# Moving the first tile's second mask ahead of the head means, and its product ahead of the head-mean product, in a macaron block on one core

## The reference

```python
x = x + 0.5 * ffn(layernorm(x))          # 8 experts, top 2 by softmax, capacity per expert
x = x + attn(layernorm(x))
x = x + 0.5 * ffn(layernorm(x))

# attn: 16 heads of 16 channels
q, k, v = split(x @ w_qkv.T)             # q and k are rotated and scaled by position
scores = (q @ k.T) * D ** -0.5 * decay_mask          # causal, gamma ** distance
y = scores @ v
mean, var = y.mean, y.var                # for each batch and head, over its 16 channels and all 1024 tokens
yn = (y - mean) / sqrt(var + eps) * gn_weight + gn_bias
out = (silu(x @ w_gated.T) * yn) @ w_proj.T
```

## Time and profile before

| | |
|---|---|
| median of 3 runs | 2312.23 us (2309.82 to 2313.85) |
| profiled execution | 2312.59 us, of which the span from first to last instruction is 2310.8 us |
| PE busy | 2170.1 us, 94% of the span |
| DVE busy | 1358.5 us, 59% |
| ACT busy | 1003.8 us, 43% |
| POOL busy | 1171.7 us, 51% |
| mean granted TensorE clock | 0.977 of full speed |

### The profile page before, as it was taken

How to read it: one execution, slowest core, us unless ns; L and a number is a source line. 1 busy time by engine, 2 the same in 40 slices (tenths; PEclk the granted TensorE clock), 3 DMA queues, 4 the chain that set the end, 5 groups by cost and what they waited for, 6 DMA issues and landing times.

```text
span 2310.8 us, 57931 instructions
## 1 busy us (share of the span) xinstructions
PE 2170.1 (94%) x22549; PEld 1907.2 (83%) x22549; DVE 1358.5 (59%) x3312; ACT 1003.8 (43%) x2149; POOL 1171.7 (51%) x911
## 2 busy tenths in 40 slices
PE   7869999999999997999999999849999999999998
PEld 6759999999999987777777777638999999999997
DVE  7755555555555552578778877645555555555553
ACT  4434434343434342446555555434344444444442
POOL 5755777735354533223344453454777654444443
PEclk9999999999999998999999999869999999999999
DMA  9523444434343424102211121123444443434432
GB/s 365 211 81 68 101 93 99 99 87 98 82 104 81 105 55 119 39 21 76 76 40 59 59 77 75 60 81 94 100 92 102 90 101 86 100 87 99 89 80 32
DMA packets 138440, 211.52 MB, mean 92 GB/s; under 512 B 34092, under 2 KB 114544, under 8 KB 132080
## 3 DMA queue, kind: packets, MB, share of 16 engines
q0 software_dynamic: 57344, 69.21, 17.9%
q1 hardware_dynamic: 80912, 139.72, 17.5%
HBM read 138.13 MB, written 72.88 MB: 91 GB/s over the span
## 4 chain that ended last, share of the span: by engine, by line
PE 52%; DVE 4%; issue 2%; ACT 1%; another core or an unknown queue 0%; POOL 0%; DMA 0%; POOLq 0%; DVEq 0%; ACTq 0%
PE bank L675 16%; PE bank L657 15%; PE bank L768 10%; PE bank L856 3%; PE bank L889 1%; PE bank L824 1%; PE bank L644 1%; PE bank L839 1%; PE bank L874 1%; PE bank L928 1%; PE bank L786 1%; DVE aw L1829 0%; DVE rt L1817 0%; DVE xnl L1803 0%
## 5 line engine op out<-in xcount | busy, mean ns | idle before, releaser
L1167 ACT ACTIVATE h<-bank 128x512 f32<-128x512 f32 x512 | 306.1, 598 | 850.9 <-PE bank L657 740.0
L1738 DVE CAST hh<-h 128x512 fp32r<-128x512 f32 x512 | 241.2, 471 | 692.6 <-ACT h L1167 578.8
L675 PE MATMUL bank<-w2h,hh 128*128 128x256 f32 x2048 | 579.1, 283 | 3.1 <-ACT yb L1185 3.1
L675 PE MATMUL bank<-w2h,hl 128*128 128x256 f32 x2048 | 573.7, 280 | 0.0
L675 PE MATMUL bank<-w2l,hh 128*128 128x256 f32 x2048 | 573.7, 280 | 0.0
L675 PEld LDWEIGHTS bank<-w2h,hh 128*128 128x128 f32 x2048 | 385.1, 188 | 45.4 <-ACT yb L1185 3.6
L675 PEld LDWEIGHTS bank<-w2h,hl 128*128 128x128 f32 x2048 | 384.8, 188 | 41.5
L675 PEld LDWEIGHTS bank<-w2l,hh 128*128 128x128 f32 x2048 | 385.2, 188 | 39.4
L657 PE MATMUL bank<-xh,w1h 128*128 128x512 f32 x1024 | 405.1, 396 | 2.0 <-issue 1.7
L657 PE MATMUL bank<-xh,w1l 128*128 128x512 f32 x1024 | 404.3, 395 | 0.0
L657 PE MATMUL bank<-xl,w1h 128*128 128x512 f32 x1024 | 404.1, 395 | 0.0
(11 more groups left out here) (215 smaller groups left out, 3305.0 us busy)
## 6 DMA issues: line engine op xcount, KB each, us to landing
stg<-in_L_ffn_w SPq DMA_DIRECT2D x64, 1024.0 KB
xb<-acc SPq DMA_DIRECT2D x9, 1024.0 KB
xa<-in_L_attn_x SPq DMA_DIRECT2D x8, 1024.0 KB, 14.4
xn_rows<-xa SPq DMA_DIRECT2D x8, 1024.0 KB
xn_rows<-xn_r SPq DMA_DIRECT2D x8, 1024.0 KB
xr<-acc SPq DMA_DIRECT2D x7, 1024.0 KB
out_rows<-xr SPq DMA_DIRECT2D x7, 1024.0 KB
slot_table<-pay,idx POOLq DMA_INDIRECT x256
```

The source lines that it names most:

```text
L675: product = pe.matmul(tile_sum(j, t, end), a[:, fj, t * P:(t + 1) * P], c[:, fj, :], start=(fj == 0 and i == 0 and (end or t % 2 == 0)), s ...
L1167: act.activation(h32[fj % 2][:], bank[fj % 2][:], ACT.Gelu_apprx_tanh).then_inc(f.gelu, 1)
L1738: dve.tensor_copy(hh[:, fj, :], h32[fj % 2][:]).then_inc(f.hh, 1)
```

## The change

Two calls change places, one on each of two engines. On PE `attend(n)` now stands ahead of `head_means(b - 1)`. On DVE `mask(n, 1)` now stands ahead of `channels(b - 1)`.

```diff
@@ def sequence(b), in the program of TensorE @@
                 turn(n + 1)
                 memory(n)
                 new_state(n + 1, 0)
+                attend(n)
                 head_means(b - 1)
-                attend(n)
                 residual_pair(b - 2, 2)
                 scores(n + 1, 0)
                 new_state(n + 1, 1)
@@ def sequence(b), in the program of VectorE @@
                 mask(n, 0)
                 channel_stats(n - 1)
                 front_stats(b + 1, 0)
+                mask(n, 1)
                 channels(b - 1)
-                mask(n, 1)
                 rotate(n + 2)
                 carry(n + 1, 0)
                 about_head(b - 1)
```

## The result

The changed kernel took 2324.44 us (median of 6 runs, 2319.77 to 2326.66), the kernel before 2310.61 us beside it (6 runs). The ratio is 1.0052, with a 95% interval of 1.0039 to 1.0065, so 9 to 15 us slower. The forecast was 2320.8 us, in a range of 2313.5 to 2327.

The account below looks back on a forecast made before the run. PE was taken to bound the kernel, other engines counting only where PE waits for them. Waits of 5.45 us at L907 plus 3.1 us of clock falls, 8.55 us, gave 2320.8 us, range 2313.5 to 2327.

Parts of the forecast that it names:

- The mask gains nothing: On DVE at batch start: the mask still starts 0.73 us after its scores (L856), gain 0, with DVE idle ahead.
- Channels in the open, 1.25 us: On DVE: channels now runs after the mask, where nothing hides it, and delays what is queued behind by 1.25 us.
- TensorE's half, 0: On PE: `attend(n)` 0.31 us earlier, head means some 0.8 us later, together taking what they took: 0.
- L1885 is held by L504: DVE's L1885 lasts until POOL's L504 ends, about 1.14 us instead of 0.16 us, before and after the change.
- the rule that was weighed: SBUF port rule: two-input Vector instructions block while GpSimd reads SBUF; without it, near 1 us of waits instead of 5.45.
- The waits, 5.45 us: PE's added waits for DVE at L907 in batches 1 to 7, each 1.25 us less the slack: 5.45 us.
- The slack: Time between L1888 and L907 above 0.22 us: 1.07, 0.80 and 1.35 us in batches 3, 5 and 6.
- The clock, two new falls behind L907, 3.1 us: PE's clock falls to half level after L907 in two more of five batches, 1.55 us each: 3.1 us.
- The rate taken: How often PE's clock falls after a wait or gap near L907: two in four, used to take two falls.
- The sum, 8.55 us: Whole kernel: waits of 5.45 us at L907 plus clock falls of 3.1 us, 8.55 us slower.
- Rival C: Waits at L907 swallowed by PE's larger slack or issue gaps: 2315 us if half goes, 2312 if all; chance 0.18.
- Rival B: Waits at L907 alone, the clock falling no more often: 2317.7 us, slower by 0.24%; chance 0.19.

Follow-up runs that it names:

- e1: DVE's half of the change alone (mask ahead of channels, TensorE's order as before) against the kernel before: 2324.27 us, ratio 1.0035.
- e2: TensorE's half of the change alone (`attend(n)` ahead of the head means, DVE as before) against the kernel before: 2318.57 us, ratio 1.0008.
- e4: The change, with POOL also waiting for L1888 before it starts `rotated(n + 2)` (L504), against the kernel before: 2321.97 us, ratio 1.0021.
- e8: The kernel before with only POOL made to wait for L1888 before `rotated(n + 2)`, against the kernel before: ratio 0.9994.
- e11: The same kernel as e4, timed again in another group against the kernel before: ratio 1.0019.
- e12: The same kernel as e8, timed again in another group against the kernel before: ratio 0.9998.
- e9: The kernel before, unaltered, timed against itself and profiled a second time: ratio 0.9997.
- e5: The change itself again on another chip (second comparison and second profile), against the kernel before: 2322.51 us, ratio 1.0035.
- e6: The change, with TensorE filling its wait at L907 with 8 unread transposes in seven batches, against the kernel before: 2322.29 us, ratio 1.0034.
- e3: The change, with `head_variances(b - 1)` moved behind `residual_pair(b - 2, 3)` and `project(n + 3)` on TensorE, against the kernel before: ratio 1.0062.

## Why the prediction was right, and where it was off

The direction was right, and so was the path by which TensorE comes to wait at L907. That the sum came close is in part luck, as the last points show.

- **The mask gains nothing.** Right: 0.74 us behind its scores, with 1.17 us of idle time of DVE ahead of it.
- **Channels in the open, 1.25 us.** Right, 1.21 measured. By e1 and e2 the loss is in this half, as far as the times can tell.
- **TensorE's half, 0.** Right in time (e2). That the two calls "take what they took" was off by 0.2 us a batch in favour of the new order, by e1's waits against those of the change. It only made the wait longer.
- **L1885 is held by L504.** Shown by e4, e8, e11 and e12 (0.16 us in every case) and by e2. For the size of the loss the rule that was weighed mattered as said: with the block gone the stretch from L856 to L907 went from 39.98 back to 34.67 us, and an undisturbed batch lost 0.19 us (4.75 for 4.56) where the rule's absence was priced at 0.2. The time of the kernel didn't follow as far: the prediction had near 1 us for that case, and e4 and e11 show 4 to 5.
- **The waits, 5.45 us.** Measured as the growth of that stretch: 5.07. The bare idle time grew by 7.3 us (7.8 less 0.5), more than forecast. The issue gaps of 0.7 to 1.0 us that stood ahead of L907 in the batches 3, 5 and 6 lie within the new waits or beside them now. The slack that I had taken from them came out as expected all the same: 5.71 against 5.57, 5.30 and 5.85 are 0.14, 0.41 and -0.13 us, where I had 0.18, 0.45 and 0.
- **The clock, two new falls behind L907, 3.1 us.** Two in the first profile (batches 5 and 7), three in the second (2, 4, 5), one in e1 (5). The estimate was good for this place. But the lost clock of the whole stretch from batch 1 grew by 6.9, 3.4 and 8.6 us in these three. Falls came at other places too, some of double length (the one of batch 1 among them), and this I had put at nothing. The rate taken, two in four, would also have given 2.5 of five and not two.
- **The sum, 8.55 us.** From batch 1 on the profile shows 8.0, but not as 5.45 and 3.1: the lost clock grew by 6.9, and the issue gaps shrank. The two misses went opposite ways. The median shows 13.8 in the first comparison and 9.2 in the second; the intervals reach from 4.9 to 15.0. The term missed is batch 0, 3.7 us in the first profile. It is a longer gap in TensorE's issue and a fall of the clock behind it, in instructions that didn't change. Since e4 and e11, one kernel, show it at 3.0 and at 1.3 us, the program's order doesn't fix it. Whether the order makes the long gap likelier stays open.

Rival C had something for it. The issue gaps of TensorE from batch 1 to the end of the stage went from 9.3 to 6.8 us, and those that stood between L856 and L907 were passed during the new waits. But the kernel before itself shows only 5.9 us in e9, so the sum alone proves nothing, and it came nowhere near to paying for the waits. Rival B, the waits alone, would have been 2317.7 us, below every execution of the first comparison. The interval of e5, 5 to 11 us, still contains its 5.45. Against it stands the clock of the executions, 0.9743 for 0.9762; but since e6 has that clock nearly back at the same time, the part of the falls in the loss isn't shown.

Two things stay open: the 4 to 5 us that e4 and e11 keep although their stretch to L907 is as before, and how much of the median is due to the falls, which e6 should have shown and didn't. No version clearly beats the kernel before.

## What to carry to other kernels

Before an instruction is moved up on its engine, look at what ends the wait of the one that moves: if its start stands at a fixed distance behind its releaser in every batch (here 0.73 us), the work ahead of it is free filling, and moving up only turns that work into delay for everything behind. A chain that crosses engines is priced where the bounding engine meets it (here 4.56 us from L856 to L907 became 5.71), not by the length of the moved work. And a product moved out of the way of a wait (e3) takes its bank along: see who claims that bank next.

## What the hardware showed that I had not expected

- A DVE instruction on 2 numbers per partition took 1.13 us beside a POOL instruction that reads SBUF, and 0.16 us without it. It only mattered once something waited for it.
- TensorE stood for 1.3 to 4.2 us in its own issue at one and the same instruction (L839, batch 0), on the same program with 1.3 in one profile and 3.0 in another. The traces show what ended these gaps. Beside the data they list packets of 16 KB, one at a time, on a queue of the kind "instruction". Of the changed kernel, from 975 to 990 us:

```profile
q1 hardware_dynamic: 1184, 2.10, 40.0%
q8 instruction: 2, 0.03, 1.0%
```

The first of the two ran from 982.58 to 983.53, and TensorE went on at 985.02. In the kernel before it ran from 980.14 to 981.08, and TensorE went on at 982.54. The 14 profiles have 66 issue gaps of TensorE over 0.6 us between 930 and 1500 us, and every one ended 1.25 to 1.59 us after such a packet had landed. So these gaps are, by all that the traces show, waits for TensorE's own program. Just ahead of the gap in batch 0 two loads of 1 MB start to move. In the nine profiles with a gap of 1.3 to 1.6 us the packet started 1.3 to 1.7 us after the first data of these loads, in the five with 3.0 to 4.2 us it started 3.2 to 4.3 us after it. Whether the loads hold the packet back, or it was asked for later, isn't shown.
- The clock's answer to the same stretch with the same wait differs from batch to batch: behind a wait of 1.3 us it fell in 3 of 6 batches in the first profile (one further fall, in batch 6, had no wait ahead of L907) and in 4 of 6 in the second.
